# A graph layer's hand-ordered VectorE program: two one-hot groups moved ahead of the reading of the sums, and one addition moved three runs later

## The chip, the cores and the metric

One core of a Trainium2 chip runs the whole program. The metric is device microseconds from start to end of one execution. Engines are named PE (TensorE), ACT (ScalarE), DVE (VectorE), POOL (GpSimd) and SP (SyncE); each runs its own list of instructions in order and waits only on semaphores.

## The reference

One message-passing layer on a graph of 12,500 nodes with 128 features and 200,000 edges (`src`, `dst`), then a residual and a layer norm:

```python
h_self   = x @ W_lin + b_lin
messages = x[dst] @ W_msg + b_msg
msg_sum  = segment_sum(messages, src, 12500)
counts   = segment_sum(ones, src, 12500)
h_agg    = msg_sum / maximum(counts, 1)[:, None]
h        = concatenate([h_self, h_agg], 1) @ W_upd + b_upd
out      = layernorm(x + relu(h))          # over the 128 features, no scale or shift
```

`dst` comes sorted, `src` is random. The sum of the messages of a node is linear in the rows of x, so the kernel sums rows of x first and multiplies once afterwards; the bias `b_msg` then enters as one constant row for every node that has any edge (`bmsg_rep` times min(count, 1)).

## The kernel before, in words

**First part** (to about 625 us; the change does not touch its instructions). The 200,000 edges are cut into 80 chunks of 2,500. Each chunk's edges are sorted into bins by the node that receives them, x is split into three bf16 parts side by side (384 columns, `F3`), and `base` = x times the joined self weights is made and stored.

**Second part** (to the end). The 12,500 receiving nodes are cut into 25 **quads** of 4 x 128 nodes (`Q` = 25). In a quad every chunk contributes up to 32 rows for each of the 4 groups of 128 nodes. 68 of the 80 chunks are *hot*: their rows lie in one, two or three windows of 128 consecutive rows of x that stay in SBUF. They are worked in 17 **runs** of 4 chunks (`RUNS`), in the order `ORDER = [7, 0, 8, 1, 15, 2, 9, ...]`; a run is two **pairs** (steps) of 2 chunks. The other 12 chunks and up to 7 spilled sets are gathered from DRAM by POOL, one quad ahead. For each run:

- DVE, `hot_windows` (L913 to L922): makes the one-hot matrices that pick rows from windows, one `tensor_scalar` per window (L919), into one of `NW_` buffers `W`. Before it writes run R it waits until PE has gathered run R - NW_.
- DVE, `hot_nodes` (L924 to L929): makes the one-hot `L` that sends each row to its node, one `tensor_tensor` (L929), into one of `NL` = 4 buffers; `hot_dma_nodes` (L937) does it for the gathered chunks.
- PE, `gather` (L1213 to L1226): 2 matmuls per window and pair into one of two PSUM slots (L1224). It waits for W and for the slot: the pair before the last must have been taken out.
- ACT, `take_rows` (L534 to L539): copies the pair's slot to SBUF (L539, 128x768).
- PE, `aggregate` (L1228 to L1240): 8 matmuls per pair add the rows into the four accumulators `acc` (L1238), one run behind `gather`; `aggregate_dma` (L1249) and `aggregate_spills` (L1257) add the gathered rows.

The order on each engine is written out by hand in loops over `q` and `r` (DVE: L1005 to L1023; PE: L1277 to L1300; ACT: L559 to L570). In DVE's loop at run r the windows and nodes of run r + 1 are made. **At a quad's change** PE gathers run 0 of the new quad, aggregates the last run of the old one, and gathers runs 1 and 2; at r = 2 it aggregates four steps at once (a group of 32 matmuls), for which the old sums must have been read out of `acc`. ACT reads two of the accumulators at r = 0 (L546), between its copies of run 0 and run 1. DVE reads the other two at r = 1 (`take_sums`, L945 to L950), then makes windows and nodes of run 2 and the DMA nodes, then does `mean` (L952 to L970): counts, the sum of the three bf16 parts, the division, and at its end four additions of the constant to `base4` (L968). `mean` sets `S_ready` for PE's transposes at r = 5 (L1265). The layer's matmul follows at r = 8 (L1274), `layer` on DVE at r = 9 (L979 to L987; it waits for `constant_added`), the root on ACT at r = 10 (L557) and `norm` on DVE at r = 11 (L992 to L999). SP loads the next quads' tables `brow` (L364), x and base.

```python
                for q in range(Q + 1):
                    for r in range(RUNS):
                        if q > 0 and r == 1:
                            take_sums(q - 1)
                        if q < Q:
                            n = q * RUNS + r + 1
                            if n < RUNS * Q:
                                hot_windows(n // RUNS, n % RUNS)
                                hot_nodes(n // RUNS, n % RUNS)
```

Of the kernel before, what the change touches and what calls it, by code (L numbers as in the profile page):

```python
# [9 lines left out]
def gnn_program(nc, x, src, dst, w_lin, b_lin, w_msg, b_msg, w_upd, b_upd, out):  # L10
# [14 lines left out]
    Q = H // 4  # L25
# [8 lines left out]
    def n_win(c):  # L34
        return 1 if c < 28 else 2 if c < 60 else 3
# [15 lines left out]
    CD = C - CP  # L51
# [17 lines left out]
    with ctx:  # L69
        def sb(name, shape, dt):  # L70
            return ctx.enter_context(nc.sbuf_tensor(name, shape, dt))
# [4 lines left out]
        def sem(name):  # L76
            return ctx.enter_context(nc.semaphore(name))

        WIN_BYTES = NWIN * F3 * 2
        AREA_BYTES = 104 * 1024  # L80
        big = sb("big", [P, (WIN_BYTES + AREA_BYTES) // 4], f32)

        def shaped(flat, text, /, **sizes):
            return flat.rearrange(text, **sizes)
# [36 lines left out]

        one_a = Area(NWIN_A * F3 * 2, WIN_BYTES + AREA_BYTES)
        OH = [shaped(one_a.take(2 * T * H, f16), "p (a h j) -> p a h j", h=H, j=2) for _ in range(3)]
# [22 lines left out]


        two = Area(WIN_BYTES, WIN_BYTES + AREA_BYTES)
        NB, NW_, NL, NX, ND = 2, 3, 4, 6, CD // 2
        brow = [two.take(CP * P, f16) for _ in range(NB)]  # L150
        W = [shaped(two.take(3 * 4 * P, bf16), "p (k n) -> p k n", k=3) for _ in range(NW_)]
        L = [shaped(two.take(4 * P, bf16), "p (a n j) -> p a n j", a=2, j=2) for _ in range(NL)]
# [13 lines left out]

        three = Area(WIN_BYTES, WIN_BYTES + AREA_BYTES)
        f_srcc, f_dstc = three.take(1, i32), three.take(1, i32)
# [65 lines left out]
        s = {n: sem("s_" + n) for n in names}  # L234
# [14 lines left out]
        RUNS = CP // 4  # L249
# [23 lines left out]
        def bc(a, n):  # L273
            return a.unsqueeze(2).to_broadcast([a.shape[0], a.shape[1], n])
# [392 lines left out]
        def _(dve):  # L667
            made = [0]

            def mark(ins):  # L670
                made[0] += 1
                ins.then_inc(s["dve_made"], 1)
                return made[0]
# [19 lines left out]
            n = mark(nc.vector.tensor_reduce(low_f[:, 1:2], dst_rows, AX.X, ALU.max))  # L693
# [4 lines left out]
            n = mark(nc.vector.tensor_copy(lh_b[:, :, :], slot[0][:, 0, 0:2 * C].rearrange("p (k c) -> p k c", c=C)))  # L698
            after(n)
            nc.vector.tensor_copy(low_g[:, SHARED[-1][1]:C], lh_b[:, 0, SHARED[-1][1]:C])  # L700
            for g, (a, b) in enumerate(SHARED):
                n = mark(nc.vector.tensor_reduce(gmin[:, g:g + 1], lh_b[:, 0, a:b], AX.X, ALU.min))
            after(n)
            for g, (a, b) in enumerate(SHARED):
                n = mark(nc.vector.tensor_copy(low_g[:, a:b], gmin[:, g:g + 1].to_broadcast([P, b - a])))
# [3 lines left out]
            n = mark(nc.vector.tensor_tensor(over[:, :], lh_b[:, 1, :], low_g[:, :], ALU.subtract))  # L709
            after(n)  # L710
            for a, b in ((0, 28), (28, 60), (60, 80)):
                n = mark(nc.vector.tensor_scalar(over[:, a:b], over[:, a:b], P * n_win(a) - 0.5, None, ALU.is_gt))
# [164 lines left out]
            n = mark(nc.vector.tensor_tensor(d_d, dm_s, lowm1[:, 60:C].unsqueeze(1).to_broadcast([P, Q, CS]), ALU.add))  # L877
# [4 lines left out]
            for q in range(Q):  # L882
                n = mark(nc.vector.max(out=spv[:, q, :], in_=sv[:, q, :]))
# [3 lines left out]
            n = mark(nc.vector.tensor_scalar(sp_f[:, :, :], spv[:, :, :], -1.0, 0.0, ALU.add, ALU.max))  # L887
# [3 lines left out]
            n = mark(nc.vector.tensor_copy(sp_i[:, :, :], sp_f[:, :, :]))  # L891
# [4 lines left out]
            n = mark(nc.vector.tensor_single_scalar(sp_i[:, :, :], sp_i[:, :, :], 7, ALU.logical_shift_right))  # L896
            after(n)
            n = mark(nc.vector.scalar_tensor_tensor(out=sp_lo[:, :, :], in0=sp_i[:, :, :], scalar=-float(P), in1=spv[:, :, :], op0=ALU.mult, op1=ALU.add))
# [8 lines left out]
            def fast():  # L907
# [5 lines left out]
                def hot_windows(q, r):  # L913
                    g, R_ = ORDER[r], q * RUNS + r
                    dve.wait_ge(brow_loaded[q % NB], 16 * (q // NB + 1))
                    if R_ >= NW_:
                        dve.wait_ge(s["gathered"], 2 * (R_ - NW_ + 1))
                    for k in range(n_win(g * 4)):
                        last = nc.vector.tensor_scalar(W[R_ % NW_][:, k, :].rearrange("p (c h n) -> p c h n", c=4, h=4),  # L919
                                                       brow[q % NB].rearrange("p (h c n) -> p c h n", h=4, n=SL)[:, g * 4:g * 4 + 4, :, :],  # L920
                                                       iota_k[:, k:k + 1], None, ALU.is_equal)
                    last.then_inc(s["W_ready"], 1)  # L922
# [29 lines left out]
                def mean(q):  # L952
                    dve.wait_ge(s["sums_taken"], 4 * (q + 1))
                    counts = acc_sb[:, :, F3]
                    k1 = mark(nc.vector.tensor_scalar(cnt[:, 0, :], counts, 1.0, None, ALU.max))
                    nc.vector.tensor_scalar(cnt[:, 2, :], counts, 1.0, None, ALU.min)
                    if q > 0:
                        dve.wait_ge(s["S_turned"], q)
                    k2 = mark(nc.vector.tensor_tensor(S, acc_sb[:, :, 0:F], acc_sb[:, :, F:2 * F], ALU.add))
                    after(k1)  # L960
                    k1 = mark(nc.vector.reciprocal(cnt[:, 1, :], cnt[:, 0, :]))
                    after(k2)
                    k2 = mark(nc.vector.tensor_tensor(S, S, acc_sb[:, :, 2 * F:F3], ALU.add))
                    after(max(k1, k2))
                    nc.vector.tensor_tensor(S, S, bc(cnt[:, 1, :], F), ALU.mult).then_inc(s["S_ready"], 1)
                    dve.wait_ge(base4_loaded[q % 2], 16 * (q // 2 + (2 if q == Q - 1 else 1)))
                    for h in range(4):
                        ins = nc.vector.scalar_tensor_tensor(out=base4[q % 2][:, h, :], in0=bmsg_rep, scalar=cnt[:, 2, h:h + 1], in1=base4[q % 2][:, h, :],  # L968
                                                             op0=ALU.mult, op1=ALU.add)
                    ins.then_inc(s["constant_added"], 1)  # L970
# [33 lines left out]
                hot_spills(0)  # L1004
                for q in range(Q + 1):  # L1005
                    for r in range(RUNS):
                        if q > 0 and r == 1:
                            take_sums(q - 1)
                        if q < Q:
                            n = q * RUNS + r + 1  # L1010
                            if n < RUNS * Q:
                                hot_windows(n // RUNS, n % RUNS)
                                hot_nodes(n // RUNS, n % RUNS)
                            if r % 4 == 1 and r < 2 * ND:
                                hot_dma_nodes(q, r // 4)
                        if q > 0 and r == 1:
                            mean(q - 1)
                        if q > 0 and r == LAYER:
                            layer(q - 1)
                        if q > 0 and r == NORM:  # L1020
                            norm(q - 1)
                        if q + 1 < Q and r == RUNS - 2:
                            hot_spills(q + 1)  # L1023
# [317 lines left out]
```

## Time and profile before

| | |
|---|---|
| time, median of 3 runs | 1679.45 us (1676.09 to 1680.61) |
| the profiled execution's own time | 1674.59 us |
| its span, first to last instruction | 1672.8 us |
| busy in the span: PE / DVE / ACT / POOL | 81% / 68% / 47% / 29% |
| one quad, from one reading of the sums to the next | about 43 us |

How to read the rows: a row of the timeline has the start in us, the time in us, the engine, the line of the kernel, the operation, output <- input with partitions x elements, and the count of instructions merged into it; in brackets stands the idle time of that engine just before, and the instruction that ended it as the profile infers it. PEld is the weight load of a matmul, which overlaps PE. A wait for two semaphores is put down to one of them only. Instructions of one engine overlap slightly in the rows.

### The profile page before, as it was taken

The numbers are of one execution on the slowest core, as the hardware profiler recorded it, in microseconds if no ns is written. First come the engines' busy times: TensorE is split into PE (matmuls) and PEld (weight loads), VectorE is DVE, ScalarE is ACT, GpSimd is POOL, SyncE is SP. The second block draws the span as 40 slices with busy tenths as digits, with TensorE's granted clock in tenths as the row PEclk, the third lists the DMA queues.
The fourth block names the chain that finished last, engine by engine and source line by source line (L and its number), as shares of the span: only waits on it lengthen the run. The fifth ranks groups of instructions, "written<-read, shape, count | busy, mean of one in ns | idle before, by whom it ended". The sixth has DMA issues, their size and how long they took to land.

```text
span 1672.8 us, 42910 instructions
## 1 busy us (share of the span) xinstructions
PE 1353.5 (81%) x16656; PEld 829.3 (50%) x16656; DVE 1141.7 (68%) x2880; ACT 782.5 (47%) x1128; POOL 482.8 (29%) x512
## 2 busy tenths in 40 slices
PE   3877767577675288999999999999999999999997
PEld 2767767577665134444444444444444444444443
DVE  7999999999998335555555555555555555555554
ACT  1222322100100156666666666666666666666664
POOL 1000000000000444444444444444444444444430
PEclk9777867655656589999999999999999999999998
DMA  5222122141000543343343333443444444333320
GB/s 88 83 83 102 68 83 92 55 118 43 5 1 4 181 131 106 108 113 107 116 113 114 111 112 116 116 118 117 118 117 118 116 117 119 116 116 118 117 50 11
DMA packets 119790, 160.60 MB, mean 96 GB/s; under 512 B 32099, under 2 KB 91552, under 8 KB 119516
## 3 DMA queue, kind: packets, MB, share of 16 engines
q1 hardware_dynamic: 95426, 110.08, 20.5%
q0 software_dynamic: 22880, 47.02, 12.2%
q8 instruction: 139, 2.28, 0.6%
q10 hardware_dynamic: 1290, 0.78, 0.2%
q14 instruction: 55, 0.45, 0.1%
HBM read 134.62 MB, written 23.21 MB: 94 GB/s over the span
## 4 chain that ended last, share of the span: by engine, by line
PE 44%; DVE 44%; issue 6%; ACT 4%; DMA 1%; DVEq 0%; SPq 0%; ACTq 0%
PE slot L1224 25%; PE acc L1238 12%; DVE big L777 5%; DVE big L757 5%; ACT big L539 4%; DVE big L919 3%; DVE big L782 3%; DVE big L788 3%; DVE big L815 2%; PE slot L1274 2%; DVE big L808 2%; PE acc L1249 2%; DVE big L968 2%; DVE big L784 2%; DVE big L929 1%
## 5 line engine op out<-in xcount | busy, mean ns | idle before, releaser
L539 ACT ACTIVATE big<-slot 128x768 bf16<-128x768 f32 x850 | 649.1, 810 | 421.4 <-PE slot L1224 382.9
L1224 PE MATMUL slot<-big 128*128 128x384 bf16 x2900 | 552.5, 328 | 90.5 <-DVE big L919 50.1
L1224 PEld LDWEIGHTS slot<-big 128*128 128x128 bf16 x2900 | 244.0, 98 | 377.9 <-DVE big L919 134.3
L625 POOL DMA_INDIRECT big<-x,dst_at x300 | 297.6, 992 | 300.3 <-PE acc L1238 172.6
L1238 PE MATMUL acc<-big 32*128 32x385 bf16 x6800 | 352.9, 325 | 0.4 <-issue 0.4
L919 DVE TENSOR_SCALAR big<-big,iota_k 128x512 bf16<-128x512 f16 x725 | 230.7, 352 | 140.8 <-PE slot L1224 128.1
L629 POOL DMA_INDIRECT big<-x,sp_i x175 | 179.0, 1023 | 280.6 <-PE acc L1257 133.0
L929 DVE TENSOR_TENSOR big<-col_lo,iota_lo 128x512 bf16<-128x512 f16 x425 | 177.8, 418 | 103.1 <-PE acc L1238 88.5
L1238 PEld LDWEIGHTS acc<-big 32*128 32x128 bf16 x6800 | 141.2, 93 | 176.4 <-issue 102.0
L1134 PE MATMUL acc<-big 125*100 125x64 f16 x1600 | 131.5, 259 | 113.7 <-DVE big L815 113.6
L1134 PEld LDWEIGHTS acc<-big 125*100 125x100 f16 x1600 | 126.2, 184 | 121.5 <-DVE big L815 121.5
L1123 PE MATMUL acc<-big,tri 125*125 125x100 f16 x1600 | 142.0, 265 | 33.0 <-DVE big L757 33.0
L620 POOL MEMSET big<- 128x4 bf16 x6 | 0.3, 96 | 553.7 <-issue 553.7
L1123 PEld LDWEIGHTS acc<-big,tri 125*125 125x125 f16 x1600 | 139.5, 188 | 34.4 <-DVE big L757 25.8
L950 DVE COPY big<-acc 128x385 f32<-128x385 f32 x50 | 25.6, 553 | 101.5 <-PE acc L1238 101.5
L777 DVE TENSOR_TENSOR big<-big 125x4000 f16<-125x4000 f16 x40 | 89.3, 2233 | 3.0 <-ACT big L469 3.0
L757 DVE TENSOR_TENSOR big<-big 125x4000 f16<-125x4000 f16 x40 | 89.3, 2234 | 0.0
L469 ACT ACTIVATE big<-acc 125x400 f16<-125x400 f32 x40 | 20.1, 503 | 145.3 <-PE acc L1123 145.3
L477 ACT ACTIVATE big<-acc 100x128 f32<-100x128 f32 x40 | 11.1, 277 | 153.5 <-PE acc L1134 153.5
L1249 PE MATMUL acc<-big 32*128 32x385 bf16 x1200 | 74.9, 322 | 0.0
L1257 PE MATMUL acc<-big 32*128 32x385 bf16 x700 | 58.5, 320 | 1.3 <-issue 1.3
L979 DVE TENSOR_TENSOR big<-big,slot 128x512 f32<-128x512 f32 x25 | 17.2, 687 | 61.8 <-PE slot L1274 61.8
(151 smaller groups left out, 1142.8 us busy)
## 6 DMA issues: line engine op xcount, KB each, us to landing
big<-rows SPq DMA_DIRECT2D x25, 2176.0 KB
x<-big SPq DMA_DIRECT2D x19, 480.0 KB, 2.8
big<-x SPq DMA_DIRECT2D x32, 192.0 KB, 2.5
big<-in_x SPq DMA_DIRECT2D x24, 256.0 KB
big<-base SPq DMA_DIRECT2D x24, 256.0 KB
out<-big SPq DMA_DIRECT2D x24, 256.0 KB
big<-in_x SPq DMA_DIRECT2D x19, 320.0 KB, 3.5
base<-big SPq DMA_DIRECT2D x19, 320.0 KB, 2.2
```

Of the source, the lines that this page charges most:

```text
L539: act.activation(xg[n % NX][:, :, 0:F3], slot[z % 2][:, :, 0:F3], ACT.Copy).then_inc(s["xg_ready"], 1)
L625: pool.indirect_dma_start(out=xg_d[:, c, 0:F3], out_offset=None, in_=x3_dram, in_offset=bass.IndirectOffsetOnAxis(ap=dst_at[:, q, c:c + 1] ...
L629: pool.indirect_dma_start(out=xg_sp[:, v, 0:F3], out_offset=None, in_=x3_dram, in_offset=bass.IndirectOffsetOnAxis(ap=sp_i[:, q, v:v + 1], ...
L757: nc.vector.tensor_tensor(OH[u % 3][0:EP, :, :, :], spread2(two_chunks(hi, u), H), tbl(iota2h[0:EP, :, :]), ALU.is_equal).then_inc(s["OH_r ...
L777: nc.vector.tensor_tensor(n, OH[u % 3][0:EP, :, :, :].rearrange("p (k a) h j -> p k a (h j)", k=2), R16[b][0:EP, :, :, :].rearrange("p k h ...
L919: last = nc.vector.tensor_scalar(W[R_ % NW_][:, k, :].rearrange("p (c h n) -> p c h n", c=4, h=4), brow[q % NB].rearrange("p (h c n) -> p ...
L929: nc.vector.tensor_tensor(L[R_ % NL][:, :, :, :], spread2(cols, P), tbl(iota_lo[:, :, :], 2), ALU.is_equal).then_inc(s["L_ready"], 1)
L1123: ins = nc.tensor.matmul(R_ps[u % 2][:, k * H:(k + 1) * H], tri16[0:EP, 0:EP], OH[u % 3][0:EP, k * TP + a, :, j], start=a + j == 0, stop=a ...
L1134: ins = nc.tensor.matmul(T_ps[u % 2][:, k * 2 * SL:(k + 1) * 2 * SL], OH[u % 3][0:EP, k * TP + a, :, j], OHSV[u % 2][0:EP, k * TP + a, :, ...
L1224: ins = nc.tensor.matmul(slot[z % 2][:, j, 0:F3], W[R_ % NW_][:, k, (c % 4) * P:(c % 4 + 1) * P], xwin[:, win_at(c) + k, :], start=k == 0, ...
L1238: ins = nc.tensor.matmul(acc[h][:, 0:F3 + 1], L[R_ % NL][rows, t % 2, :, j], xg[n % NX][rows, j, 0:F3 + 1], start=t == 0 and j == 0, stop= ...
L1249: ins = nc.tensor.matmul(acc[h][:, 0:F3 + 1], L_d[D_ % NL][rows, d % 2, :, j], xg_d[rows, 2 * d + j, 0:F3 + 1], start=False, stop=False)
```

## The change

`AREA_BYTES` grows by 2 KiB and `W` gets a fourth buffer (`NW_` from 3 to 4). On DVE at r = 1 of every quad that has a quad before it and is not the extra last turn, `hot_windows` of runs 2 and 3 come before `take_sums`, and are left out of their old places (r = 1 and r = 2); `hot_nodes` of these runs stay where they were. The four additions of the constant leave `mean` and become `add_constant`, called at r = 4 after that turn's windows and nodes.

```diff
-        AREA_BYTES = 104 * 1024
+        AREA_BYTES = 106 * 1024
...
-        NB, NW_, NL, NX, ND = 2, 3, 4, 6, CD // 2
+        NB, NW_, NL, NX, ND = 2, 4, 4, 6, CD // 2
...
                     nc.vector.tensor_tensor(S, S, bc(cnt[:, 1, :], F), ALU.mult).then_inc(s["S_ready"], 1)
+
+                def add_constant(q):
+                    dve.wait_ge(s["S_ready"], q + 1)
                     dve.wait_ge(base4_loaded[q % 2], 16 * (q // 2 + (2 if q == Q - 1 else 1)))
                     for h in range(4):
...
                     for r in range(RUNS):
+                        if q > 0 and r == 1 and q < Q:
+                            hot_windows(q, 2)
+                            hot_windows(q, 3)
                         if q > 0 and r == 1:
                             take_sums(q - 1)
                         if q < Q:
                             n = q * RUNS + r + 1
                             if n < RUNS * Q:
-                                hot_windows(n // RUNS, n % RUNS)
+                                if q == 0 or r not in (1, 2):
+                                    hot_windows(n // RUNS, n % RUNS)
                                 hot_nodes(n // RUNS, n % RUNS)
...
                         if q > 0 and r == 1:
                             mean(q - 1)
+                        if q > 0 and r == 4:
+                            add_constant(q - 1)
```

## Rows read from the trace of the kernel before

**Rows 1.** The page: busy time of the engines, and the span in 40 slices.
```profile
PE 1353.5 (81%) x16656; PEld 829.3 (50%) x16656; DVE 1141.7 (68%) x2880; ACT 782.5 (47%) x1128; POOL 482.8 (29%) x512
```

**Rows 2.** Stretches: start:end, length, busy us (instructions) of each engine, granted clock, DMA.
```profile
1016.70:1059.70 43.00, 38.98 (x477) 18.68 (x477) 24.62 (x78) 27.44 (x39) 18.86 (x20) 1.00 0.40 114
629.80:1658.80 1029.00, 932.93 (x11416) 447.43 (x11414) 588.19 (x1868) 658.34 (x914) 440.51 (x438) 1.00 0.38 109
```

**Rows 3.** Waits, 800 to 1640 us: total us, times, longest us.
```profile
PE slot L1224 <- DVE big L919: 32.4, 44, 1.0
PE slot L1224 <- ACT big L539: 24.0, 33, 1.0
```

**Rows 4.** Timeline of PE, 1000 to 1050 us.
```profile
1005.62 0.33 PE L1257 MATMUL acc<-big 32*128 32x385 bf16 x4
1005.88 0.82 PE L1224 MATMUL slot<-big 128*128 128x384 bf16 x4
...
1012.25 1.47 PE L1224 MATMUL slot<-big 128*128 128x384 bf16 x8
...
1016.61 0.83 PE L1224 MATMUL slot<-big 128*128 128x384 bf16 x4
1018.45 1.51 PE L1224 MATMUL slot<-big 128*128 128x384 bf16 x8 [1.01 <-DVE big L919]
1019.89 1.50 PE L1238 MATMUL acc<-big 32*128 32x385 bf16 x32
1021.22 0.33 PE L1257 MATMUL acc<-big 32*128 32x385 bf16 x4
1022.53 0.82 PE L1224 MATMUL slot<-big 128*128 128x384 bf16 x4 [0.98 <-DVE big L919]
...
1024.39 2.12 PE L1224 MATMUL slot<-big 128*128 128x384 bf16 x12
```

**Rows 5.** Timeline of DVE, 1000 to 1050 us.
```profile
1016.73 1.02 DVE L950 COPY big<-acc 128x385 f32<-128x385 f32 x2 [3.92 <-PE acc L1238]
1017.67 0.63 DVE L919 TENSOR_SCALAR big<-big,iota_k 128x512 bf16<-128x512 f16 x2
1018.22 0.41 DVE L929 TENSOR_TENSOR big<-col_lo,iota_lo 128x512 bf16<-128x512 f16 x1
...
1021.08 1.13 DVE L968 SCALAR_TENSOR_TENSOR big<-AB,cnt,big 128x128 f32<-128x128 f32 x4
1022.13 0.34 DVE L919 TENSOR_SCALAR big<-big,iota_k 128x512 bf16<-128x512 f16 x1
1022.39 0.42 DVE L929 TENSOR_TENSOR big<-col_lo,iota_lo 128x512 bf16<-128x512 f16 x1
1022.73 1.02 DVE L919 TENSOR_SCALAR big<-big,iota_k 128x512 bf16<-128x512 f16 x3
```

**Rows 6.** Timeline of ACT, 1000 to 1050 us.
```profile
1017.48 1.52 ACT L539 ACTIVATE big<-slot 128x768 bf16<-128x768 f32 x2
1019.29 1.52 ACT L539 ACTIVATE big<-slot 128x768 bf16<-128x768 f32 x2 [0.29 <-PE slot L1224]
1023.07 1.51 ACT L539 ACTIVATE big<-slot 128x768 bf16<-128x768 f32 x2 [2.26 <-PE slot L1224]
```

**Rows 7.** Timeline of PE's weight loads, 1000 to 1050 us.
```profile
1019.12 0.45 PEld L1224 LDWEIGHTS slot<-big 128*128 128x128 bf16 x4 [0.25 <-issue]
```

**Rows 8.** Timeline of PE: groups of 32 matmuls of a quad's change, second and last-but-one.
```profile
676.12 1.49 PE L1238 MATMUL acc<-big 32*128 32x385 bf16 x32
...
1621.41 1.50 PE L1238 MATMUL acc<-big 32*128 32x385 bf16 x32
```

**Rows 9.** Timeline of POOL, 1007 to 1050 us.
```profile
1012.28 0.95 POOL L625 DMA_INDIRECT big<-x,dst_at  x1 [1.40 <-PE acc L1238]
...
1025.28 1.41 POOL L625 DMA_INDIRECT big<-x,dst_at  x1 [1.64 <-PE acc L1249]
```

**Rows 10.** Waits of SP's DMA queue.
```profile
SPq L364 <- DVE big L919: 100.3, 23, 26.8
```

## The prediction

> **What bounds the kernel now.** I read the page first. PE is the busiest engine [rows 1], and its slices are full only in the second part, so I read that part by stretches. A quad takes 43.0 us, in which PE is busy 38.98, ACT 27.44, DVE 24.62 and POOL 18.86, with the full clock granted (1.00) [rows 2]. So PE paces the quads, and what a change is worth there is what it takes out of PE's remaining idle time, 4.0 us a quad. The list of waits says who ends it: DVE's window one-hots (L919) 32.4 us and ACT's copies of the slots 24.0 us over the 20 quads between 800 and 1640 us [rows 3]. DVE's part is two waits at each quad's change, just under 1 us each: PE stands 1.01 us ahead of the gather of run 2 and 0.98 us ahead of that of run 3 [rows 4]. The pattern repeats with little change: the groups of 32 matmuls of the second and of the 24th change are (1621.41 - 676.12) / 22 = 42.97 us apart [rows 8].
>
> DVE's timeline explains the names. It is idle for 3.92 us ahead of reading the sums, since it waits for the last aggregation of the old quad; it reads them from 1016.73, makes run 2's windows until 17.67 + 0.63 = 1018.30, then node one-hots and the mean, then the four additions of the constant (1.13 us from 1021.08), and only then run 3's window (1022.13 + 0.34 = 1022.47) [rows 5]. PE starts run 3 at 1022.53 [rows 4], right behind it.
>
> **The first wait is not DVE's alone.** Run 2 also needs a free slot, which ACT gives by copying the pairs of run 1. ACT does so from 1017.48, two copies in 1.52 us [rows 6]; at half each the first ends near 1018.25 to 1018.3 and the second at 1019.00. Window and slot come within 0.05 us of each other. And the second pair of run 2 starts at 1019.12 [rows 7], 0.12 us behind ACT's second copy, with its windows long made. So even if the first pair could start earlier, the second could not, and the 32 matmuls behind it at 1019.89 stay where they are. ACT's copies follow its own reading of the sums, which the change leaves alone. Gain from moving run 2's windows: 0 (bounds: 0, and 1.0 us a change if ACT were not there).
>
> **The second wait goes.** Behind the spill group at 1021.22 PE could start run 3 at once. Where nothing is late the same sequence is 1005.62 to 1005.88, so 0.26 us; here it is 1021.22 to 1022.53, 1.31 us [rows 4]. 1.31 - 0.26 = 1.05 us. Is the slot free? ACT has taken both pairs of run 2 by 19.29 + 1.52 = 1020.81 and then stands idle 2.26 us for PE [rows 6]. Yes. I take 1.05; the idle time that the row itself names, 0.98, is the lower bound, since the slot, the node one-hots and the gathered pair behind it are ready too.
>
> **What the change adds ahead of the sums.** Three window one-hots, 0.63 + 0.34 us [rows 5], in DVE's idle 3.92 us. Run 3's window now waits, with four buffers, for the gather of the old quad's last run (R - 4), the 8 matmuls from 1012.25 to 1013.72 [rows 4]. DVE is then done by about 1014.2, and it can read the sums only from 1016.73. Margin 2.5 us; cost nothing. If that cover were gone, `take_sums` would come up to 0.97 us late, and PE needs the sums only at 1019.89, 2.1 us after DVE's reading ends at 1017.75.
>
> **What is late next.** Behind the sums DVE saves run 2's windows: the nodes of run 2 start at 1017.67 in place of 1018.22. From there to the end of the mean it takes 21.08 - 18.22 = 2.86 us [rows 5], so it ends at 1020.53; nodes of run 3 take 22.73 - 22.39 = 0.34, to 1020.87; run 4's three windows 1.02, to 1021.89. PE now wants them at 24.39 - 1.05 = 1023.34 [rows 4]: a margin of 1.45 us where before it was 24.39 - 23.75 = 0.64. The constant (1.13 us) comes two runs later, behind windows and nodes of run 5, at about 1023, when DVE is ahead of PE by more than a run; behind it stand the windows of run 6, which PE gathers some 6 us later, and nothing waits for the constant before `layer` at r = 9. Cost nothing. The transposes at r = 5 get the mean 0.55 us earlier, but wait for ACT's slot, which moves with PE. All other waits of the quad (ACT's copies, the layer's slot) are chains that begin and end on PE, so they shift as a whole.
>
> **Queues.** No instruction and no DMA is added. SP's load of the next table but one waits for the count of window groups (23 times, 100.3 us in all [rows 10]); that count is reached no later, and the table is not read until more than half a quad after. POOL waits on PE's progress, a quad ahead of use. The fourth buffer lifts the wait of the windows for the gather; the node one-hots' own wait is then always the later one, so nothing in the steady runs becomes later.
>
> **Sum.** 24 changes (the 25th, behind the last quad, has no windows to make, and there the constant keeps its place behind the mean with nothing between): 24 x 1.05 = 25.2 us. Against the profiled execution, 1674.59 - 25.2 = 1649.4. That execution lies 4.9 us below the median of the runs shown, 1679.45, which is what I have to forecast: **1654.3 us**, 1.5% faster. Bounds of the known terms: 24 x 0.98 = 23.5 to 25.2. Within 0.3% (5 us), about what a measurement of this kernel can tell, I call it no change.
>
> **A place where rows and a rule meet.** DVE's window one-hots and POOL's gather issues run side by side in the trace; one issue, at 1025.28, takes 1.41 us in place of 0.95 while DVE works without a pause, and one starts at 1012.28, about where the moved windows will stand [rows 9]. The rule of the Trainium skill, page "SBUF — State Buffer", on the port pair that VectorE and GpSimd share, is that "the loser fully blocks" for the length of the other's instruction; by it each moved window could start up to one issue late. That is the second rival below; its price there is from rows.
>
> **Rivals.**
>
> 1. *Both waits go.* If PE's first wait were DVE's alone, the change would give two times 1.0 us: 24 x 2.05 = 49 us, about 1630. The rows name DVE for it in this quad, which speaks for; ACT's copies at 1018.3 and 1019.00 speak against. Chance 0.04.
>
> 2. *POOL holds DVE up.* Two issues of 0.95 us [rows 9] in the way ahead of run 4's windows would take 1.90 us, more than the margin of 1.45: PE would wait 0.45 there, the gain falls to 0.60 a change, 14.4 us, 1665. A single one costs nothing. Against it: no window group in [rows 5] shows a stretch of that size (0.34 each), and POOL issues once or twice in the 6 us of a change. Chance 0.07, for this or any other partly returned gain.
>
> 3. *The gain comes back in the same quad.* PE arrives 1 us early at a resource that does not depend on PE, such as a gathered pair or a table, and waits there. Then the time is 1679, no change; this is also the case if the wait on the window were named wrongly and something else held PE at 1022.53. Against: no wait of PE or DVE on a DMA stands among the waits of the second part, and DMA share is 0.40 [rows 2]. Chance 0.04.
>
> 4. *Slower: the layout.* The fourth buffer moves every tile behind W by 3 KiB, and no row shows what an address does to a duration. If ACT's copy of 0.81 us from such a PSUM slot to a moved tile took longer, PE would feel it at its slot waits: those of the gathers are 33 in 20 quads by name [rows 3], and with the second pair of run 2, the transposes and the layer I count about five a quad. To end over 0.3% slower the copies must eat 25.2 + 5.0 = 30 us, 1.25 us a quad, so 0.25 us each, a third longer; with that, 1685. For it speaks no row. Chance 0.03.
>
> **Chances.** Forecast 0.82, rivals 0.04, 0.07, 0.04, 0.03. Faster: 0.82 + 0.04 + 0.07 = 0.93; same 0.04; slower 0.03. The range of 8 in 10 takes the bounds of the sum, the spread of the runs shown (3.4 us below the median, 1.2 above) and reaches up to the second rival: 1646 to 1665.
>
> **What would show it.** PE's wait ahead of run 3's gather is gone, its distance from the spill group 0.26 us; the first wait is still about 1.0 us, now named for ACT; DVE shows three window one-hots between 2 and 4 us ahead of its reading of the sums, and the four additions some 6 us behind it; groups of 32 matmuls 41.92 us apart. Wrong if the first wait shrinks (rival 1), if a new wait stands ahead of run 4 (rival 2), or later in the quad (rival 3), or if ACT's copies are no longer 0.81 us (rival 4).

## The result, and the profile after

The changed kernel takes **1662.12 us** (median of 4 runs, 1659.49 to 1663.77) against 1680.03 us for the kernel before on the same chip (4 runs, 1676.09 to 1680.99): ratio 0.9896, 95% interval 0.9875 to 0.9917, 17.9 us faster. Forecast were 1654.3 us and 25.2 us. The direction and the range (1646 to 1665) held; the gain is 0.7 of the one predicted.

The page's first part after the change, which answers to [rows 1]:

```profile
PE 1352.0 (81%) x16656; PEld 829.0 (50%) x16656; DVE 1131.1 (68%) x2880; ACT 783.1 (47%) x1128; POOL 474.1 (29%) x512
```

The same instructions and, within 2%, the same busy times: what was gained is idle time. Line numbers behind the new function have moved: the gather of a run is now L1233 (it was L1224), the aggregation L1247 (L1238), the transposes L1274 (L1265), the layer's matmuls L1283 (L1274). The spans of the two profiled executions (1672.8 and 1662.0 us) differ by only 10.8 us, since the second part happens to begin later in the one after: its first group of 32 matmuls behind a quad's change starts at 638.49 in place of 632.93 us. So I go by the quads. The timeline of PE after, as [rows 8]:

```profile
681.01 1.49 PE L1247 MATMUL acc<-big 32*128 32x385 bf16 x32
...
1612.07 1.50 PE L1247 MATMUL acc<-big 32*128 32x385 bf16 x32
```

(1612.07 - 681.01) / 22 = 42.32 us a quad; before it was 42.97, and 41.92 was forecast. 0.65 us a quad came in, and 24 x 0.65 = 15.6 us; the 17.9 of the medians lies within the runs' spread of that (ratio 0.9917 at the upper end is 13.9 us).

PE's timeline at the quad's change, 1000 to 1050 us, to be laid beside [rows 4]:

```profile
1018.15 1.51 PE L1233 MATMUL slot<-big 128*128 128x384 bf16 x8 [1.01 <-ACT big L539]
1019.60 1.50 PE L1247 MATMUL acc<-big 32*128 32x385 bf16 x32
1020.92 0.33 PE L1266 MATMUL acc<-big 32*128 32x385 bf16 x4
1021.19 0.82 PE L1233 MATMUL slot<-big 128*128 128x384 bf16 x4
...
1023.04 2.12 PE L1233 MATMUL slot<-big 128*128 128x384 bf16 x12
1025.10 0.84 PE L1247 MATMUL acc<-big 32*128 32x385 bf16 x16
...
1026.03 0.82 PE L1233 MATMUL slot<-big 128*128 128x384 bf16 x4
1028.38 0.66 PE L1274 MATMUL slot<-ident,big 128*128 128x128 f32 x4 [1.52 <-ACT big L539]
```

The wait ahead of run 3 is gone (1020.92 to 1021.19, 0.27 us). The first wait is still 1.01 us and is now put down to ACT. Nothing waits ahead of run 4 (1023.04). But 7 us behind the change PE stands 1.52 us ahead of the transposes. In the trace of before the same place reads, in PE's timeline and in ACT's:

```profile
1026.45 0.84 PE L1238 MATMUL acc<-big 32*128 32x385 bf16 x16
...
1027.38 0.82 PE L1224 MATMUL slot<-big 128*128 128x384 bf16 x4
1029.13 0.66 PE L1265 MATMUL slot<-ident,big 128*128 128x128 f32 x4 [0.93 <-ACT big L539]
```

```profile
1028.27 1.51 ACT L539 ACTIVATE big<-slot 128x768 bf16<-128x768 f32 x2 [0.91 <-PE slot L1224]
```

and ACT's after:

```profile
1027.51 1.51 ACT L539 ACTIVATE big<-slot 128x768 bf16<-128x768 f32 x2 [1.50 <-PE slot L1233]
```

The transposes need the slot that this copy frees. Before, ACT began it 1028.27 - 1027.38 = 0.89 us behind the start of PE's four gather matmuls; after, 1027.51 - 1026.03 = 1.48 us, though it had been idle for 1.50 us and PE's matmuls take the same time. This quad is the largest case: over the 23 quads from the first change on the distance at this place is 1.48 us once and 1.09 to 1.19 us in the others, against 0.88 to 0.91 before. The waits tell what it comes to. PE's waits of 800 to 1640 us after (total us, times, longest), for [rows 3]:

```profile
PE slot L1233 <- ACT big L539: 37.3, 54, 1.0
PE slot L1274 <- ACT big L539: 23.3, 20, 1.5
...
PE slot L1233 <- DVE big L919: 2.1, 4, 0.5
```

and, of the kernel before, the one ahead of the transposes, which [rows 3] doesn't show:

```profile
PE slot L1265 <- ACT big L539: 18.5, 20, 1.0
```

Ahead of gathers PE's waits fall from 32.4 + 24.0 = 56.4 to 37.3 + 2.1 = 39.4 us, 0.85 a quad where 0.98 was to go; ahead of the transposes they rise by 23.3 - 18.5 = 4.8 us, 0.24 a quad. The window's wait is gone, and a bit over a third of its worth (0.40 of 1.05 us) is given back later in the same quad, at waits that are named for ACT.

DVE's timeline of after, for [rows 5]:

```profile
1012.42 0.62 DVE L919 TENSOR_SCALAR big<-big,iota_k 128x512 bf16<-128x512 f16 x2
1013.55 0.35 DVE L919 TENSOR_SCALAR big<-big,iota_k 128x512 bf16<-128x512 f16 x1 [0.50 <-PE slot L1233]
1016.43 1.02 DVE L950 COPY big<-acc 128x385 f32<-128x385 f32 x2 [2.53 <-PE acc L1247]
...
1020.59 0.87 DVE L919 TENSOR_SCALAR big<-big,iota_k 128x512 bf16<-128x512 f16 x3
...
1022.31 1.14 DVE L971 SCALAR_TENSOR_TENSOR big<-AB,cnt,big 128x128 f32<-128x128 f32 x4
...
1026.72 0.42 DVE L929 TENSOR_TENSOR big<-col_lo,iota_lo 128x512 bf16<-128x512 f16 x1 [1.81 <-PE acc L1247]
```

The moved windows end at 1013.90, 2.53 us ahead of the sums; run 4's windows end at 1021.46, 1.6 us ahead of PE's 1023.04; the constant stands 5.9 us behind the sums. The last row matters below: DVE too resumes late at run 5, 1026.72 - 1025.10 = 1.62 us behind the start of the aggregation it waits for.

### The profile page after: what moved, and what is told of

Its sections match the earlier page's. It is cut to its first block, busy times and chain, and to the rows that moved or that the text cites. A ratio compares the mean times of both kernels' runs of the same rounds, so it can differ in the third digit from the quotient of the medians.

```text
span 1662.0 us, 42934 instructions
## 1 busy us (share of the span) xinstructions
PE 1352.0 (81%) x16656; PEld 829.0 (50%) x16656; DVE 1131.1 (68%) x2880; ACT 783.1 (47%) x1128; POOL 474.1 (29%) x512
## 4 chain that ended last, share of the span: by engine, by line
PE 55%; DVE 31%; ACT 7%; issue 6%; DMA 1%; DVEq 0%; ACTq 0%; SPq 0%
PE slot L1233 30%; PE acc L1247 16%; ACT big L539 7%; DVE big L777 5%; DVE big L757 5%; DVE big L782 3%; DVE big L788 3%; PE acc L1258 2%; PE slot L1283 2%; DVE big L815 2%; PE acc L1266 2%; DVE big L808 2%; DVE big L784 2%; PE slot L1274 1%; DVE big L814 1%
## 5 line engine op out<-in xcount | busy, mean ns | idle before, releaser
L1233 PE MATMUL slot<-big 128*128 128x384 bf16 x2900 | 553.0, 329 | 67.2 <-ACT big L539 46.9
L1233 PEld LDWEIGHTS slot<-big 128*128 128x128 bf16 x2900 | 244.1, 98 | 353.6 <-issue 177.5
L625 POOL DMA_INDIRECT big<-x,dst_at x300 | 292.2, 974 | 288.9 <-PE acc L1247 173.6
L1247 PE MATMUL acc<-big 32*128 32x385 bf16 x6800 | 352.5, 325 | 0.0
L1247 PEld LDWEIGHTS acc<-big 32*128 32x128 bf16 x6800 | 141.0, 93 | 175.6 <-issue 101.3
```

The lines of the kernel that those rows point to most:

```text
L625: pool.indirect_dma_start(out=xg_d[:, c, 0:F3], out_offset=None, in_=x3_dram, in_offset=bass.IndirectOffsetOnAxis(ap=dst_at[:, q, c:c + 1] ...
L1233: ins = nc.tensor.matmul(slot[z % 2][:, j, 0:F3], W[R_ % NW_][:, k, (c % 4) * P:(c % 4 + 1) * P], xwin[:, win_at(c) + k, :], start=k == 0, ...
L1247: ins = nc.tensor.matmul(acc[h][:, 0:F3 + 1], L[R_ % NL][rows, t % 2, :, j], xg[n % NX][rows, j, 0:F3 + 1], start=t == 0 and j == 0, stop= ...
```

## The experiments

I call **lag** the distance from the start of a group of gather matmuls on PE to the start of ACT's copy of its first pair, where ACT stands idle for it. At run 3, a gather of the same size, it is 0.54 us in the median of every kernel. The four places named below are those of runs 5, 7, 10 and 11. The quad is the mean distance of the groups of 32 matmuls from the first change to the 24th, and the lags are medians over the quads from the second on, both from the profiled execution's timelines. Times are medians of 4 to 10 runs; ratios are against the kernel before, run beside each on the same chip.

| kernel | quad, us | lags at runs 5, 7, 10, 11 | time, us | ratio, 95% |
|---|---|---|---|---|
| before (first runs) | 42.98 | 0.90, 1.38, 1.06, 1.50 | 1680.03 | 1 |
| after (first runs) | 42.33 | 1.15, 1.44, 1.10, 1.59 | 1662.12 | 0.9896 (0.9875 to 0.9917) |
| windows_only | 42.36 | 1.16, 1.44, 1.10, 1.59 | 1663.88 | 0.9896 (0.9879 to 0.9912) |
| constant_only | 41.96 | 0.54, 1.70, 1.10, 1.58 | 1655.44 | 0.9852 (0.9835 to 0.9868) |
| fourth_buffer_only | 43.14 | 0.82, 1.42, 1.11, 1.57 | 1684.33 | 1.0023 (1.0011 to 1.0034) |
| after_no_gathers | 40.54 | 0.54, 0.54, 0.86, 0.54 | 1620.38 | 0.9640 (0.9624 to 0.9656) |
| before_no_gathers | 41.56 | 0.54, 0.54, 0.86, 0.54 | 1644.75 | 0.9778 (0.9749 to 0.9806) |
| after_spaced | 42.57 | 0.54, 0.54, 0.86, 0.54 | 1665.00 | 0.9884 (0.9849 to 0.9919) |
| constant_spaced | 42.46 | 0.54, 0.54, 0.86, 0.54 | 1664.41 | 0.9888 (0.9859 to 0.9917) |
| before_spaced | 43.13 | 0.54, 0.54, 0.86, 0.54 | 1683.31 | 1.0008 (0.9995 to 1.0021) |
| constant_spread * | 40.67 | 0.54, 0.54, 0.86, 0.54 | 1620.03 | 0.9876 (0.9859 to 0.9892) |
| before_spread * | 41.72 | 0.54, 0.54, 0.86, 0.54 | 1644.21 | 1.0029 (1.0015 to 1.0042) |
| constant_spread_again * | 40.67 | 0.54, 0.54, 0.86, 0.54 | 1620.93 | 0.9885 (0.9867 to 0.9904) |
| after_again * | 40.54 | 0.54, 0.54, 0.86, 0.54 | 1617.44 | 0.9870 (0.9853 to 0.9887) |

windows_only to after_no_gathers ran on one chip, before_no_gathers and the spaced kernels on another. The rows with a star ran on two other chips, where **the kernel before itself takes 1640.5 and 1640.0 us** in place of the 1680 to 1684 of the others. Their times can be read against their own kernel before alone.

### Either half alone

**windows_only**: the changed kernel, with the constant back behind the mean.

```diff
                         if q > 0 and r == 1:
                             mean(q - 1)
-                        if q > 0 and r == 4:
                             add_constant(q - 1)
```

> Only the windows are moved (with the fourth buffer); the constant stays at the end of the mean. Theory A (either half alone removes PE's wait ahead of run 3, because that wait was behind mean + constant + window): run 3's window is made ahead of the sums, run 4's three windows are then ready about 0.1 us before PE wants them (17.37 + 2.88 + 1.05 + 0.34 + 1.02 = 22.66 to 22.9 against 23.04 in the quad shown), so the quad takes 42.3 us as with the whole change and the time is 1662 +- 3 us. Rival (each half carries its own share): the quad takes about 42.6 us, 1671 us.

Measured: 1663.88 us (1662.67 to 1665.47), as the whole change. With the windows early, it is all one whether the constant stands ahead of run 4's windows or behind.

**constant_only**: the later constant, with three window buffers and the windows in their old places.

```diff
-        AREA_BYTES = 106 * 1024
+        AREA_BYTES = 104 * 1024
...
-        NB, NW_, NL, NX, ND = 2, 4, 4, 6, CD // 2
+        NB, NW_, NL, NX, ND = 2, 3, 4, 6, CD // 2
...
-                        if q > 0 and r == 1 and q < Q:
-                            hot_windows(q, 2)
-                            hot_windows(q, 3)
...
-                                if q == 0 or r not in (1, 2):
-                                    hot_windows(n // RUNS, n % RUNS)
+                                hot_windows(n // RUNS, n % RUNS)
```

> Only the constant is moved; three buffers, windows in their old places. Theory A: run 3's window follows the mean directly, 1021.08 + 0.34 = 1021.42 in the quad shown of before, where PE could start at 1021.48; so the wait is gone or under 0.1 us, the quad takes 42.3 to 42.4 us and the time is 1662 to 1665 us. Rival (the windows have to go ahead of the sums): a wait of 0.5 us or more stays ahead of run 3, the time is 1670 us or more.

Measured: 1655.44 us (1655.23 to 1657.51), 8.4 us less than windows_only on the same chip. So one half is enough to take the wait ahead of run 3 away, and this half beats both kernels, which was not expected. Its PE timeline at run 5:

```profile
1021.18 0.84 PE L1243 MATMUL acc<-big 32*128 32x385 bf16 x16
...
1022.12 0.82 PE L1229 MATMUL slot<-big 128*128 128x384 bf16 x4
1023.52 0.66 PE L1270 MATMUL slot<-ident,big 128*128 128x128 f32 x4 [0.58 <-ACT big L539]
```

its ACT timeline, and its waits of 800 to 1640 us:

```profile
1022.65 1.51 ACT L539 ACTIVATE big<-slot 128x768 bf16<-128x768 f32 x2 [0.55 <-PE slot L1229]
```

```profile
PE slot L1229 <- ACT big L539: 38.1, 49, 1.0
PE slot L1270 <- ACT big L539: 11.5, 20, 0.6
```

Here ACT starts 0.53 us behind PE's group, and the wait ahead of the transposes costs 11.5 us in 20 quads: 11.8 less than after the change, 0.59 a quad; run 7's lag grows to 1.70 and takes part of it back. What is different? POOL's timeline is; here are that of constant_only and that of after:

```profile
1020.65 1.68 POOL L625 DMA_INDIRECT big<-x,dst_at  x1 [1.16 <-PE acc L1254]
1022.64 0.94 POOL L625 DMA_INDIRECT big<-x,dst_at  x1 [0.30 <-PE acc L1262]
```

```profile
1024.59 1.14 POOL L625 DMA_INDIRECT big<-x,dst_at  x1 [1.11 <-PE acc L1258]
1026.03 0.95 POOL L625 DMA_INDIRECT big<-x,dst_at  x1 [0.30 <-issue]
```

POOL's second gather issue starts 0.52 us behind PE's group of run 5 in constant_only and exactly with it, at 1026.03, in after. In the kernel before it starts at 1026.99, 0.39 us ahead of the group. The quad of after is the exception there; in its other quads the issue starts about 0.28 us ahead of the group, as in the next one (PE, ACT and POOL), with a lag of 1.12 us:

```profile
1068.67 0.82 PE L1233 MATMUL slot<-big 128*128 128x384 bf16 x4
1069.79 1.51 ACT L539 ACTIVATE big<-slot 128x768 bf16<-128x768 f32 x2 [1.14 <-PE slot L1233]
1068.38 0.95 POOL L625 DMA_INDIRECT big<-x,dst_at  x1 [0.30 <-PE acc L1247]
```

And where ACT is late, DVE is too: behind the start of the same aggregation its next node one-hots begin 1.62 us later in after, 0.89 in constant_only (at 1022.07), 1.07 before (at 1027.52). Two engines that wait for different semaphores resume late together, so it is PE's signals that arrive late, not ACT that is slow. (The ends of PE's matmuls are modelled in the profile, but their starts tell against a slow PE: in after DVE resumes 0.69 us behind the start of the group that follows the awaited aggregation, at 1026.03; before it is 0.14 us.)

**fourth_buffer_only**: the kernel before, with four window buffers and nothing else.

```diff
-        AREA_BYTES = 104 * 1024
+        AREA_BYTES = 106 * 1024
...
-        NB, NW_, NL, NX, ND = 2, 3, 4, 6, CD // 2
+        NB, NW_, NL, NX, ND = 2, 4, 4, 6, CD // 2
```

> The kernel before with the fourth buffer and 2 KiB more area, no instruction moved. Theory A: PE's two waits of 1.0 us at the quad's change stay, the quad takes 42.97 us, the time is that of before within 0.3%. Rival (the layout or the deeper ring itself gives or costs): ACT's copy is not 0.81 us or the quad differs by over 0.1 us.

Measured: 1684.33 us, 0.23% slower (0.11 to 0.34), so 4 us, 6 at most; the wait ahead of run 3 stays. What is longer is single quads, and with the late signal: three take 43.8 us, and in these three alone the lag at run 5 is 1.6 us, where it is 0.80 to 0.95 in the others, whose lengths are 42.95 to 43.17. So no row shows that the layout itself costs anything.

### Without POOL's gathers

The theory by now: POOL's gather issues delay PE's signals. **after_no_gathers** and **before_no_gathers** leave the gathers of all quads but the first out, so that PE adds that quad's rows again in each; nothing else is touched. The issues go and their transfers with them. The edit, made to each kernel:

```diff
-                for q in range(Q):
+                for q in range(1):
...
-                    pe.wait_ge(pair_loaded[d], 32 * (q + 1))
+                    pe.wait_ge(pair_loaded[d], 32)
...
-                    pe.wait_ge(spill_loaded[v], 16 * (q + 1))
+                    pe.wait_ge(spill_loaded[v], 16)
```

> The changed kernel, with POOL's gathers of all quads but the first left out (PE aggregates the rows of the first quad again and again). In the changed kernel ACT starts the copy of run 5's first pair 1.5 us after PE's group starts, where 0.54 is usual, and those of runs 7 and 11 likewise; PE waits 1.52, 0.47 and 0.53 us behind them. Theory B: PE's signals reach the others late there because POOL issues two gathers close together; without gathers ACT starts 0.54 us after PE everywhere, the three waits shrink by 0.9 to 1.0, 0.47 and 0.53 us, the quad takes about 40.4 us and the time is about 1616 us. Rival C (the delay is ACT's own, or PE's): the three delays stay, the quad takes 42.3 us, the time is 1662 us.

Measured: 1620.38 us (1619.42 to 1621.71), all four lags down, a quad of 40.54 us. So POOL's gathers cost PE 42.36 - 40.54 = 1.8 us a quad (the first number is that of windows_only, on the same chip), though PE nowhere waits for one.

> The kernel before, with POOL's gathers of all quads but the first left out, the partner of after_no_gathers (1620.4 us, quad 40.5 us). Theory B (the change takes 1.05 us off every quad's change, and it is POOL's gathers that give a part of it back at run 5): without gathers the change is worth its full 1.05 us, so this kernel takes 1620.4 + 25.2 = 1645.6 us, quad 41.6 us. Rival C (the change was never worth more than 0.65 us a quad): 1636 us, quad 41.2 us.

Measured: 1644.75 us (1644.06 to 1646.40). The difference of the two is **24.4 us**, and that of their quads 1.02 us: with the signals on time the change is worth all but 0.8 us of the forecast 25.2. The two ran on different chips, on which the kernel before takes 1683.91 and 1681.96 us; less that difference it is 22.4 us. The quads, 40.51 and 41.53 us in all but the first of each, within 0.01 us, are the firmer number. Its waits of 800 to 1640 us and those of after_no_gathers show the swap that the prediction described, one of two waits going and the other keeping its 1.0 us:

```profile
PE slot L1224 <- ACT big L539: 20.3, 20, 1.0
PE slot L1224 <- DVE big L919: 19.1, 20, 1.0
PE slot L1265 <- ACT big L539: 11.5, 20, 0.6
```

```profile
PE slot L1233 <- ACT big L539: 19.3, 19, 1.0
PE slot L1274 <- ACT big L539: 11.5, 20, 0.6
```

The first kernels' own traces hold the same comparison, with nothing edited. POOL gathers a quad ahead, so the last quad has no issue beside it: in the kernel before the last one starts at 1618.15. At run 5 of that quad PE and ACT read

```profile
1628.87 0.82 PE L1224 MATMUL slot<-big 128*128 128x384 bf16 x4
1629.40 1.51 ACT L539 ACTIVATE big<-slot 128x768 bf16<-128x768 f32 x2 [0.55 <-PE slot L1224]
```

a lag of 0.53 us where the 23 quads ahead of it show 0.88 to 0.91. In the last quad the other three places, and all four in after, show the lags of the kernels without gathers too.

### Gathers put elsewhere

If the issues delay the signals, their place should decide. The **spaced** kernels let POOL wait for a gather of PE in place of an aggregation, so that its issues begin at other points of the runs:

```diff
-                            pool.wait_ge(s["aggregated"], (q - 1) * STEPS + int(GAP * i) + 1)
+                            pool.wait_ge(s["gathered"], (q - 1) * STEPS + [6, 8, 10, 12, 14, 16, 18, 20, 22, 24, 26, 28, 30, 31, 32, 34, 35, 36, 38][i] + 1)
```

> The changed kernel; each of POOL's 19 gathers of a quad now waits for a pair of its own that PE has gathered (steps 6, 8, 10, ... 38), so that they are issued 2 us or more apart wherever PE also signals gathered rows, and about 25 us ahead of their use. Nothing is left out. Theory B (two issues close together make PE's signals late): the late copies of runs 5, 7 and 11 are rarer or gone, the quad takes 40.6 to 41.6 us, the time is 1620 to 1645 us. Rival D (any gather issue near PE's signals delays them, however spaced): the quad stays at 42.0 to 42.6 us, 1655 to 1668 us.

> The kernel with only the constant moved, and POOL's gathers spaced as in after_spaced. Theory B: as after_spaced, 1620 to 1645 us, since the position of DVE's work no longer decides where two issues meet. Rival D: 1650 to 1660 us.

> The kernel before with POOL's gathers spaced as in after_spaced. Theory B: it lies 24 x 1.05 = 25 us above after_spaced, since PE's wait ahead of run 3 is back and nothing gives a part of the gain back any more. Rival C: 16 to 18 us above it.

Measured: 1665.00 us (1658.59 to 1669.04), 1664.41 (1661.93 to 1666.14) and 1683.31 (1682.41 to 1685.49). The lags at the four places vanish in all three, and the time does not: a miss. PE's timeline of after_spaced shows why:

```profile
1015.63 1.51 PE L1233 MATMUL slot<-big 128*128 128x384 bf16 x8 [0.46 <-ACT big L539]
...
1020.54 2.70 PE L1233 MATMUL slot<-big 128*128 128x384 bf16 x8 [1.88 <-issue]
```

The three issues that now stand back to back there are in POOL's:

```profile
1016.71 0.95 POOL L629 DMA_INDIRECT big<-x,sp_i  x1 [0.73 <-PE slot L1233]
1017.96 0.95 POOL L625 DMA_INDIRECT big<-x,dst_at  x1 [0.31 <-issue]
1019.22 0.95 POOL L625 DMA_INDIRECT big<-x,dst_at  x1 [0.30 <-issue]
```

New delays stand at the end of the old quad and at the change, where before there were none: PE's first wait is 1.88 us in place of 1.01. Moving the gathers moves the late signals along. The change is worth 1683.31 - 1665.00 = 18.3 us here, again less than the 25 that were expected (the four runs of after_spaced lie 10 us apart; by the quads it is 0.56 us).

The **spread** kernels differ from these in the list alone: [6, 8, 10, 12, 14, 16, 18, 18, 20, 22, 24, 26, 26, 28, 30, 32, 34, 36, 38], which leaves the end of a quad less crowded.

> Only the constant moved; POOL's 19 gathers of a quad are tied to gathered pairs again, but none sits in the quad's change: steps 6, 8, 10, 12, 14, 16, 18, 18, 20, 22, 24, 26, 26, 28, 30, 32, 34, 36, 38. In after_spaced the late copies of pairs 10, 14, 20 and 22 were gone (all 0.54 us or 0.86 behind PE's group), but those of pair 32 and of the reading of the sums came 0.9 us late, where three issues in a row stood. Theory B2 (a gather issue holds PE's signals until about 0.4 us behind its end; it costs time only where the held signal is one that the chain waits for): all these copies are on time, the quad takes 40.6 to 41.3 us, the time is 1622 to 1640 us, below every kernel so far that does all the work. Rival D (the gathers cost 1.4 us a quad wherever they stand): the quad stays at 41.9 us or more, 1655 us or more.

> The kernel before with the same placing of POOL's gathers. Theory B2 with the step of the prediction (PE's wait ahead of run 3 is worth 1.05 us a change): 24 x 1.05 = 25 us above constant_spread. Rival C (0.65 us a change): 16 us above it.

Measured: 1620.03 us (1618.95 to 1621.24) and 1644.21 (1641.44 to 1646.46), with no late signal left. Read alone, that is the cure. But the kernel before took 1640.52 us beside them, so the chip was another one, and there before_spread is even 0.29% slower than the kernel before. The new places are not what made them fast. Between these two kernels the constant alone is worth 24.2 us, 1.01 a quad.

**constant_spread_again** and **after_again** are the same kernel as constant_spread and the changed kernel itself, unedited, to separate chip from placement.

> The same kernel as constant_spread, since its first run came on another chip than the runs before it, one on which the kernel before takes 1640.5 us and not 1682. Theory B2 (placing the gathers keeps the held signals off the chain, on any chip): where the kernel before takes about 1680 us, this one takes 1622 to 1640 us. Theory E (what made constant_spread fast was the chip, on which PE's signals are not held at all; placing gains nothing): where the kernel before takes about 1680 us, this one takes 1650 us or more. Where the kernel before takes about 1640 us again, both give 1620 us and nothing is decided between them.

> The changed kernel unchanged, beside constant_spread_again. Theory F (the change is worth 1.0 us a quad where PE's signals are not held, and 0.65 us where they are): where the kernel before takes about 1640 us this one takes 24 x 1.02 = 24.5 us less, 1616 us; where it takes about 1680 us, 16 to 19 us less, 1662 us. Rival (the part given back at run 5 has nothing to do with the held signals): 16 to 19 us less on either.

Measured: 1620.93 us (1618.63 to 1621.66) and 1617.44 (1616.33 to 1618.79). The kernel before took 1639.99 us (1636.93 to 1642.87). So the chip was again one of the faster kind, and whether the new places would help on the others stays undecided. But the unedited changed kernel does as well as any. Busy times of 800 to 1600 us (columns as [rows 2]), of after_again, which gathers, of after_no_gathers on the other chip, which doesn't, and of the changed kernel's first profile, there with its gathers:

```profile
800.00:1600.00 800.00, 764.14 (x9424) 371.25 (x9416) 475.52 (x1525) 540.65 (x749) 364.87 (x360) 1.00 0.41 115
```

```profile
800.00:1600.00 800.00, 764.18 (x9411) 371.60 (x9408) 473.24 (x1539) 540.15 (x749) 0.00 (x0) 1.00 0.21 71
```

```profile
800.00:1600.00 800.00, 735.15 (x9005) 352.71 (x8998) 457.38 (x1478) 518.89 (x719) 354.48 (x360) 1.00 0.40 116
```

In the first two PE does the same work in the same time, with POOL busy for 364.87 us or for none; in the third, at the same DMA share as in the first, it gets 29 us less done. The granted clock is 1.00 in all, so neither it nor the DMA load tells the chips apart. Of after_again at run 5, PE's and ACT's timelines:

```profile
1003.34 0.82 PE L1233 MATMUL slot<-big 128*128 128x384 bf16 x4
1004.74 0.66 PE L1274 MATMUL slot<-ident,big 128*128 128x128 f32 x4 [0.58 <-ACT big L539]
```

```profile
1003.87 1.51 ACT L539 ACTIVATE big<-slot 128x768 bf16<-128x768 f32 x2 [0.55 <-PE slot L1233]
```

and POOL's:

```profile
1001.24 1.52 POOL L625 DMA_INDIRECT big<-x,dst_at  x1 [0.46 <-issue]
1003.06 0.95 POOL L625 DMA_INDIRECT big<-x,dst_at  x1 [0.30 <-PE acc L1247]
1004.32 0.95 POOL L629 DMA_INDIRECT big<-x,sp_i  x1 [0.30 <-issue]
```

Three issues in a row lie around the group, one of them beginning 0.28 us ahead of it, just as in after, and the signal is on time all the same (0.53 us; in after it was 1.12). On this chip gather issues don't delay PE's signals. The change is worth 1639.99 - 1617.44 = 22.6 us there, 0.94 a quad, of the 24.5 that were expected if the loss comes from the late signals and the 16 to 19 if it doesn't (the ratio's interval is 18.5 to 24.1 us, so the medians alone only just exclude the second).

A count over all kept traces with gathers puts the cases together. It takes the copies that ACT, standing idle, makes of a pair from the third quad on. Where nothing is late, ACT starts 0.36 us behind the start of the pair's last matmul; I call that moment *due*, and *late* what comes over 0.1 us behind it. On the slower chips (eight traces, 2964 copies, 525 late):

- 264 are due 0.3 to 1.25 us behind the start of an issue that itself follows another within 0.35 us. All 264 are late, by 0.26 to 1.20 us. Another 23, among them those of run 5 of constant_only, are due less than 0.3 us behind such a start, and none of these is late.
- Behind the start of an issue that stands alone, none of the 334 that are due within 0.7 us is late, but 224 of the 343 that are due 1.0 to 1.3 us behind it are, by up to 1.72 us.
- The other 37 late ones are late by 0.20 us at most.

On the two faster chips (four traces, 1472 copies) 238 lie as the 264 do, and not one of the 1472 is late.

## Why the prediction was right, and where it was too large

*PE paces the quads, and what counts is its idle time.* Right: busy times stand, the quads got shorter.

*The first wait stays, since ACT ends it too.* Right, and visible wherever the gathers are in their old places: 1.01 us, named for ACT once the window is early. constant_only, which leaves run 2's windows where they were, loses nothing by it (1.02 us there, named for DVE): moving those is worth 0.

*The second wait goes, 1.05 us a change.* Right as a mechanism. In the two kernels without gathers it is 1.02 us, in the two spread ones 41.72 - 40.67 = 1.05.

*The moved windows hide in DVE's idle time, and run 4's windows keep a margin of 1.45 us.* Right: 2.53 and 1.6 us. The constant comes three runs later, not two as the working says, and at 1022.31, close to the 1023 expected. Rival 2 fails by its own mechanism; part of the gain does come back, as the words at its chance (0.07) allowed, but not there and not through DVE. Of the rule about the port pair (the Trainium skill, "SBUF — State Buffer", section "Terms": "the loser **fully blocks**") the traces show POOL's issues stretched beside DVE, 1.14 us in after and 1.68 in constant_only for 0.95. DVE's window one-hots beside an issue take up to 0.43 us in after and 0.50 before, away from one 0.36 at most: stretched too, but none by the length of an issue.

*"All other waits of the quad … are chains that begin and end on PE, so they shift as a whole."* **This is the step that failed**, and with it the size of the second term: 0.65 us a quad in place of 1.05. The chain from PE's gather of run 5 to ACT's copy and back to PE's transposes has a link whose length depends on where POOL's issue falls. On the first chip it was late before the change too, 0.90 us in place of 0.54 in the median, so the trace held the warning: PE's wait ahead of the transposes was 0.93 us, and I took it for a constant. With DVE and PE a microsecond earlier, POOL's issue and PE's group met differently (the lag rose to 1.15), and about 0.4 us a quad went back. That the loss comes with the gathers on such chips is shown by the two kernels without them (1.02 us a quad between them, against 0.65) and by the last quad of the first traces. That a signal is late by where it falls beside the issues is shown by the count above. That this is the issue's doing and not its transfer's follows from these places, not from a run that has one without the other; and the place doesn't set the whole size, since in fourth_buffer_only the issue 0.38 us ahead of the group goes with a lag of 0.95 us in some quads and 1.6 in three.

That the time fell within the range owes something to luck. The range reached to 1665 for the sake of rival 2, POOL holding DVE up, which didn't happen; another loss of nearly the same size did. On the chip of after_again the same forecast of the gain would have been off by 2.6 us only (22.6 of 25.2).

*Rivals 1, 3, 4.* The first wait did not go. No resource outside PE took all the gain. No copy became longer (1.51 to 1.52 us for two). With the layout alone the kernel is 0.23% slower (0.34 at most), and that time stands in quads with a later signal.

## What to carry to other kernels

Where a change shortens one engine's wait, look at the hand-offs behind it that are longer than the same hand-off elsewhere in the loop (here 0.90 and 1.50 us against 0.54): they depend on something that is not in the chain and need not shift with it, so the gain should be forecast with a lower bound that lets them grow. Try the halves of a change apart: here moving the constant alone, without a fourth buffer and without moving a window, took 1655.4 us where the whole took 1662 to 1664. That holds for the chips with late signals; where none is late the whole is not behind (1617.4 us, and 1620.0 and 1620.9 for the constant alone with its gathers spread). And when kernels are compared over several sessions, run the kernel before beside each: without it, constant_spread would have been credited with 60 us that belong mostly to the chip.

## What had not been expected of the hardware

PE's signals can reach their waiters late without PE's matmuls changing: ACT resumed 0.54 us behind a group's start in one place and 1.70 us (a median; 2.26 once in windows_only) in another, DVE with it. On the slower chips this costs 43.0 - 41.6 = 1.4 us a quad before the change and 42.3 - 40.5 = 1.8 after. It goes when POOL's gathers are left out (1684 to 1645 us for the kernel before, 1662 to 1664 down to 1620 for the changed one), and moves when they move. Late are the signals due 0.3 to 1.25 us behind the start of an issue that follows another at once (264 of 264), and many of those due 1.0 to 1.3 us behind one that stands alone (224 of 343).

Chips differ in it. The kernel before takes 1680 to 1684 us (medians) on some and 1640 on two others, 2.5% less, and the changed kernel's trace from one of these has every lag at its floor with all gathers done. The kernel before has no trace from there, only its times. What in a gather issue holds the signals, why only on some chips, and whether any placement of the gathers would help on those, stays open: the two placements were tried on different chips.
